# A hyperbolic attention layer: VectorE's per-unit flag, bound and product shifted one step ahead of its copies

## Chip, cores and metric

One Trainium2 chip, one core. The metric is the device time of one execution in microseconds (us). The kernel before ran three times: 2008.18, 2013.67 and 2014.71 us, median 2013.67.

## The reference

The input is x, 8 sequences of 1024 tokens with 256 features, in float32. The layer computes

```python
def _L0_attn_ref(x, W_q, W_k, W_v, W_o, log_c, beta, attention_bias):
    q_h = exp_map_at_origin(split_heads(x @ W_q.T), c)      # 16 heads of 16
    k_h = exp_map_at_origin(split_heads(x @ W_k.T), c)
    v_h = exp_map_at_origin(split_heads(x @ W_v.T), c)
    dist = poincare_distance(q_h, k_h, c)   # arccosh(max(1 + 2c|q-k|^2 / max((1-c|q|^2)(1-c|k|^2), EPS), 1 + EPS))
    weights = softmax(-beta_pos * dist - attention_bias)
    out = einsum('bhst,bhtd->bhsd', weights, log_map_at_origin(v_h, c))
    return concat(log_map_at_origin(exp_map_at_origin(out, c), c)) @ W_o.T
...
x = x + _L0_attn_ref(_layernorm(x), ...)
x = x + fp8_gemm(_layernorm(x)) + bias      # input and weights rounded to float8_e4m3
```

The denominator of the distance is bounded from below by EPS = 1e-5. For most pairs of head and tokens that bound is what holds, and then the distance depends on the product of q and k alone.

## The kernel before

**Steps and units.** The attention is cut into 512 steps. A group G (0 to 15) is 512 query tokens of one sequence; it has 32 steps s: 4 sets of 4 heads (hg) by 8 tiles of 128 keys (kt). Step n = 32 G + s computes one matrix of 128 keys by 4 x 512 queries. Four steps in a row are a unit. Before each unit ScalarE and VectorE each read a flag from `a.opens` into a register and branch on it. A unit whose flag is 0 is closed (the bound EPS holds for all its pairs), one whose flag is 1 is open. With these inputs 12 steps, three units, are open.

**ScalarE.** In a step it does a logarithm over 128x2048 (`log(n)`, L1053 from PSUM in a closed step, L1048 from SBUF in an open one) and, one step later in its order, an exponential (L1060) in place. Nothing else of weight runs on it in the loop.

**VectorE in an open step.** `bound(n)` (L1120, four operations of 128x512) writes the bounded factors into the ring U and counts up `m_rdy`; `clamp(n)` (L1129, 128x2048) multiplies them by the products of q and k in PSUM and counts up `freed`. `log(n)` waits for that, and so does TensorE with its next products. In a closed unit VectorE only counts `m_rdy` up by four.

**VectorE in every step.** It also copies what TensorE has put into PSUM bank 7 and works off pieces of two pipelines: `project` (layer norm, q, k, v and their maps, for a group two ahead) and `finish` (output projection and the fp8 layer, for the group before). Which piece belongs to which step is a table of slots: `PROJECT_USES` and `FINISH_USES` for the fills of bank 7, the `k ==` cases of the two `vector` functions for the pieces. Slots of `project` run four steps ahead of s, those of `finish` are s itself. So in groups 1 to 13 the steps 3 to 9 and 11 fill bank 7 with the products M0 to M7 (L394, copied by L481). Step 6 has the copy of M3 and then eleven short operations of `finish`, each of which waits for the one before (the last is L730). Steps 2, 10, 18 and 26 have the sums of a set of heads (`normalise`, L1143 to L1153). Step 18 has also the short pieces L609 to L613, step 19 the product L616. Step 22 ends in L750, which is waited for; step 23 copies R2 (L489) and then reduces A0 (filled by L404), both in bank 7, one behind the other.

**TensorE.** Its order in step n is: products of q and k for steps n+1 and n+2 (L947; they wait for `freed` of `log(n)`), first half of the step's fill of bank 7, the value products of step n-1 (L962), second half of the fill. Bank 7 is one bank: each fill waits until VectorE has copied the one before.

**The flag.** On VectorE it is this passage, once in four steps, between the pieces of a step with s = 3 modulo 4 and those of the next:

```python
o = opened(n0)
v.wait_ge(a.open_rdy, flags_of(n0))
hold(v, passed_v)
is_open = v.value_load(a.opens[0:1, o:o + 1], min_val=0, max_val=1)
with v.If(is_open > 0):
```

A group's flags are computed on VectorE itself, in step 27 of the group two earlier (step 2 for group 1, step 30 of group 0 for group 2). SyncE waits on `m_rdy` before it loads the factors of the next set of heads (`load_rq`, 1 MB, once in eight steps); closed steps don't read them.

Of the kernel before, what the change touches and what calls it, by code (L numbers as in the profile page):

```python
# [32 lines left out]
KT = S // P  # L33
# [6 lines left out]
STEPS = HG * KT  # L40
N = NG * STEPS
UNIT = 4
# [65 lines left out]
def hold(eng, passed):  # L108
    eng.sem_inc(passed, 1)
# [172 lines left out]
def at(table, slot, half):  # L282

    return [key for key, where in table.items() if where == (slot, half) or (half, where) == (1, (slot, BOTH))]
# [495 lines left out]
def emit_layer(nc, g):  # L780

    with ExitStack() as ctx:
# [24 lines left out]
        def in_step(G, s, half):  # L807

            found = []
            if s % KT == SUM_STEPS % KT and half == 0:  # L810
                x = HG * G + (s - SUM_STEPS) // KT
                if 0 <= x < NG * HG and G < NG:
                    found.append(("S", x // HG, x % HG))
            found += [(kind, n, i) for n, k in finished(G, s) for kind, i in at(FINISH_USES, k, half)]
            found += [(kind, n, i) for n, k in projected(G, s) for kind, i in at(project_uses(n), k, half)]
            if G == 0:
                found += [(kind, 1, i) for kind, i in at(FIRST_USES, s, half)]
            return found

        def projected(G, s):  # L820

            slots = [(2, k) for k in ([], [], [0, 1], [2, 3])[s]] if G == 0 and s < 4 else [(2, STEPS * G + s)]
            slots += [(n, STEPS * (G + 2 - n) + s + EARLY) for n in range(3, NG)]
            return [(n, k) for n, k in slots if 0 <= k < PROJECT_SLOTS]

        def project_uses(n):
            return SECOND_USES if n == 2 else PROJECT_USES

        def finished(G, s):

            return [(n, k) for n, k in ((G - 2, s + STEPS), (G - 1, s)) if n >= 0 and 0 <= k < FINISH_SLOTS]
# [14 lines left out]
        for key in tail:  # L846
            uses.add(key)

        project = project_stage(nc, ctx, g, a, uses)
        finish = finish_stage(nc, ctx, g, "fi_", on, a.b7_filled, a.b7_copied, uses)  # L850
        a.x1 = finish.xt
        flat = finish.sq[:, :, :, :].rearrange("p t h d -> p (t h d)")
        setup = setup_stage(nc, ctx, g, U[:, 0:2].rearrange("p r h q -> p (r h q)"), finish.xb[:, 0:2, :],
                            flat[:, 0:2 * D], flat[:, 2 * D:], finish.ocT[:, 0, :])
        KERNEL_STEP = 12

        def split(n):

            return n // STEPS, (n % STEPS) // KT, n % KT
# [5 lines left out]
        def place(n, h):  # L865

            return (h + 2) % HPG if n % 2 else h

        def chunk(n):
            return g.ps[:, 2 * (n % 2):2 * (n % 2) + 4, :].rearrange("p b n -> p (b n)")  # L870

        def opened(n):

            G, hg, kt = split(n)
            return (G * 2 + kt // UNIT) * HG + hg

        def flags_of(n):

            G, hg, kt = split(n)
            return max(G, 2 * (G // 2) + kt // UNIT) + 1  # L880

        with nc.Block() as block:
# [227 lines left out]
            def _(v):  # L1110
# [3 lines left out]
                def bound(n):  # L1114

                    G, hg, kt = split(n)
                    if n >= RING:
                        v.wait_ge(pv_done, n - RING + 1)
                    for h in range(HPG):
                        ins = v.tensor_scalar(U[:, n % RING, place(n, h), :], rqb[:, h, :],  # L1120
                                              a.rk[:, (G // 2) % 2, hg * HPG + h, kt:kt + 1],
                                              1.0 / EPS, ALU.mult, ALU.min)
                    ins.then_inc(m_rdy, 1)

                def clamp(n):
                    v.wait_ge(m_rdy, n + 1)
                    v.wait_ge(d_rdy, n + 1)
                    all4 = U[:, n % RING].rearrange("p b n -> p (b n)")
                    v.tensor_tensor(all4, all4, chunk(n), ALU.mult).then_inc(freed, 1)  # L1129

                def copy_sums(x):
                    v.wait_ge(pv_done, KT * (x + 1))
                    if x >= 1:
                        v.wait_ge(a.b7_filled, uses.after(("S", (x - 1) // HG, (x - 1) % HG)))
                    v.tensor_copy(OTs[:, :], g.ps[:, 6, :]).then_inc(ot_done, 1)  # L1135

                def normalise(G, hg):
                    x = HG * G + hg
                    step = Steps(v, sum_steps, 2 * x)
                    pairs = g.ps[:, 7, :].rearrange("p (a r) -> p a r", r=2 * VW)  # L1140
                    sums = pairs[:, :, DH:DH + 2 * NS].rearrange("p a (b r) -> p a b r", b=2)
                    v.wait_ge(a.b7_filled, uses.after(("S", G, hg)))
                    step(v.tensor_reduce(den[:, :].rearrange("p (a b) -> p a b", b=2), sums, AX.X, ALU.add))  # L1143
                    v.tensor_reduce(cm[:, x:x + 1], pairs[:, :, DH:DH + 2 * NS], AX.XY, ALU.max)
                    step(v.reciprocal(den[:, :], den[:, :]))
                    for odd in range(2):
                        v.tensor_tensor(on[:, :, hg * HPG + odd:(hg + 1) * HPG:2, :],
                                        pairs[:, :, odd * (2 * VW - DH):odd * (2 * VW - DH) + DH].rearrange(
                                            "p (t c) r -> p t c r", t=GT),
                                        den[:, odd::2].rearrange("p (t c) -> p t c", t=GT).unsqueeze(3).broadcast_to(  # L1150
                                            [P, GT, HPG // 2, DH]), ALU.mult).then_inc(on_done, 1)
                    v.wait_ge(on_done, 2 * x + 2)
                    v.sem_inc(a.b7_copied, 1)  # L1153

                def copy(kind, n, i):
                    if kind == "S":
                        normalise(n, i)
                    elif (kind, i) in FINISH_USES:
                        finish.copy(v, n, (kind, i))
                    else:  # L1160
                        project.copy(v, n, (kind, i))

                def unit(n0, is_open):
                    for n in range(n0, n0 + UNIT):
                        G, s = n // STEPS, n % STEPS
                        if is_open and n + 1 < n0 + UNIT:
                            bound(n + 1)
                            clamp(n + 1)
                        for key in in_step(G, s, 0):
                            copy(*key)  # L1170
                        for key in in_step(G, s, 1):
                            copy(*key)
                        if n % KT == 0 and n >= KT:
                            copy_sums(n // KT - 1)
                        for m, k in finished(G, s):
                            finish.vector(v, m, k)
                        for m, k in projected(G, s):
                            project.vector(v, m, k)
                        if n == KERNEL_STEP:
                            setup.vector_kernel(v)  # L1180

                for k in range(3):
                    project.vector(v, 0, k, first)
# [7 lines left out]
                for n0 in range(0, N, UNIT):  # L1191
# [3 lines that stand above are left out]
                    is_open = v.value_load(a.opens[0:1, o:o + 1], min_val=0, max_val=1)  # L1195
                    with v.If(is_open > 0):
                        v.wait_ge(rqb_in, 16 * (n0 // KT + 1))
                        bound(n0)
                        clamp(n0)
                        unit(n0, True)  # L1200
                    with v.Else():
                        v.sem_inc(m_rdy, UNIT)
                        unit(n0, False)
                copy_sums(NG * HG - 1)
                normalise(LAST, HG - 1)
                for m, k in after:
# [262 lines left out]
```

## Time and profile before

| | |
|---|---|
| median of three runs | 2013.67 us |
| the profiled execution, its own time | 2004.81 us |
| its span, first to last instruction | 2003.0 us |
| mean granted TensorE clock | 0.973 |
| ScalarE busy | 1871.1 us, 93% |
| TensorE (matmul) busy | 1776.1 us, 89% |
| VectorE busy | 1139.9 us, 57% |
| start of the first and of the last logarithm (L1053) | 45.2 and 1942.8 us |

The span runs from the first instruction to the last; the execution's own time is 1.8 us longer. Shares are means over the span. An engine can be busy for 57% of it and still be what the others wait for in some steps.

### The profile page before, as it was taken

To read this page: it belongs to the slowest core of one execution; us is meant where nothing else is said; L and a number is where in the kernel's file an instruction comes from. 1 tells how busy PE (TensorE), PEld (TensorE's weight loads), DVE (VectorE), ACT (ScalarE), POOL (GpSimd) and SP (SyncE) were. 2 spreads that over 40 slices of the span, in tenths; PEclk is the share of its full clock that TensorE was granted. 3 is DMA by queue.
4 is the path that set the end of the run, shared out by engine and by line. 5 is a ranking of instruction groups with operands and counts; after the bars stand their busy time and mean duration, and the time that the engine had idled before them with its cause. 6 is when DMAs were issued, how large, how long until landed. Compare 5 with 4: busy or idle time off the path is not lost. (4 is left out here: it accounts for less than half of the span.)

```text
span 2003.0 us, 29496 instructions
## 1 busy us (share of the span) xinstructions
PE 1776.1 (89%) x10689; PEld 593.9 (30%) x10689; DVE 1139.9 (57%) x2813; ACT 1871.1 (93%) x1090; POOL 14.3 (1%) x35
## 2 busy tenths in 40 slices
PE   7888989999898798989898898999989899999982
PEld 4222322323232232323222232232323223333321
DVE  7463665655565765655657666565656556323435
ACT  5799999999999699999998999999999999999990
POOL 2000000000000000000000000000000000000000
PEclk9799999999999899999999999999999999999995
DMA  1323122041313114122030412204131220412001
GB/s 56 111 93 106 46 97 79 22 133 43 118 37 101 53 43 133 27 96 75 25 130 22 133 43 87 89 23 133 43 113 42 101 64 22 123 43 64 22 22 32
DMA packets 112937, 142.53 MB, mean 71 GB/s; under 512 B 35676, under 2 KB 61533, under 8 KB 112733
## 3 DMA queue, kind: packets, MB, share of 16 engines
q1 hardware_dynamic: 112732, 140.13, 22.2%
q8 instruction: 89, 1.46, 0.3%
q14 instruction: 116, 0.94, 0.2%
HBM read 85.07 MB, written 55.05 MB: 70 GB/s over the span
## 5 line engine op out<-in xcount | busy, mean ns | idle before, releaser
L1060 ACT ACTIVATE U<-U 128x2048 f32<-128x2048 f32 x512 | 1003.1, 1961 | 0.3
L1053 ACT ACTIVATE U<-ps 128x2048 f32<-128x2048 f32 x500 | 961.8, 1924 | 29.6 <-PE ps L947 22.6
L947 PE MATMUL ps<-q_T,k_T 18*128 18x512 f32 x4096 | 628.0, 644 | 134.4 <-ACT U L1053 108.8
L962 PE MATMUL ps<-U,vals 128*32 128x512 f32 x4096 | 555.0, 614 | 29.2 <-ACT U L1060 28.9
L947 PEld LDWEIGHTS ps<-q_T,k_T 18*128 18x128 f32 x4096 | 196.7, 185 | 349.9 <-ACT U L1053 274.2
L394 PE MATMUL ps<-wT,xnT 128*128 128x384 f32 x512 | 228.1, 537 | 4.7 <-DVEq L1153 2.5
L481 DVE COPY qkv<-ps 128x384 f32<-128x384 f32 x112 | 62.4, 557 | 220.0 <-PE ps L394 220.0
L962 PEld LDWEIGHTS ps<-U,vals 128*32 128x32 f32 x4096 | 81.2, 109 | 197.4 <-ACT U L1060 136.8
L985 PE MATMUL ps<-woT,ident 128*128 128x256 f32 x396 | 138.9, 432 | 0.0
L394 PEld LDWEIGHTS ps<-wT,xnT 128*128 128x128 f32 x512 | 79.4, 190 | 194.6 <-issue 109.5
L399 PE MATMUL ps<-ident,rows 128*128 128x128 f32 x512 | 106.6, 305 | 5.9 <-DVE rows L616 3.6
L489 DVE COPY q_T<-ps 128x512 f32<-128x512 f32 x60 | 41.5, 691 | 120.3 <-PE ps L399 120.3
L399 PEld LDWEIGHTS ps<-ident,rows 128*128 128x128 f32 x512 | 54.0, 144 | 179.5 <-issue 129.9
L985 PEld LDWEIGHTS ps<-woT,ident 128*128 128x128 f32 x396 | 59.1, 188 | 159.1 <-issue 146.2
L491 DVE COPY k_T<-ps 128x512 f32<-128x512 f32 x60 | 41.5, 691 | 69.9 <-PE ps L399 69.6
L1135 DVE COPY OTs<-ps 128x512 f32<-128x512 f32 x64 | 43.8, 684 | 65.3 <-PE ps L962 65.3
L682 PE MATMUL ps<-woT,fi_ocT 128*128 128x256 f32 x256 | 75.4, 421 | 1.6 <-DVE fi_ocT L704 0.8
L1143 DVE TENSOR_REDUCE den<-ps 128x16 f32<-128x256 f32 x64 | 27.2, 424 | 70.7 <-PE ps L971 70.1
L682 PEld LDWEIGHTS ps<-woT,fi_ocT 128*128 128x128 f32 x256 | 45.7, 198 | 54.8 <-issue 25.1
L710 DVE TENSOR_TENSOR fi_x<-fi_xt,ps 128x512 f32<-128x512 f32 x32 | 22.0, 688 | 64.8 <-PE ps L682 64.8
L572 DVE TENSOR_REDUCE ss<-sqr 128x48 f32<-128x768 f32 x56 | 53.4, 953 | 1.9
L571 DVE TENSOR_TENSOR sqr<-qkv 128x768 f32<-128x768 f32 x56 | 53.1, 948 | 0.0
(178 smaller groups left out, 1138.5 us busy)
## 6 DMA issues: line engine op xcount, KB each, us to landing
rqb<-q_scratch SPq DMA_DIRECT2D x64, 1024.0 KB, 5.6
q_scratch<-q_T SPq DMA_DIRECT2D x16, 1024.0 KB, 4.6
k_scratch<-k_T SPq DMA_DIRECT2D x16, 1024.0 KB, 6.8
v_scratch<-vals SPq DMA_DIRECT2D x16, 768.0 KB, 10.8
fi_xt<-in_L_attn_x_dram SPq DMA_DIRECT2D x17, 512.0 KB, 5.5
out_dram<-fi_x SPq DMA_DIRECT2D x16, 512.0 KB, 3.9
xt<-in_L_attn_x_dram SPq DMA_DIRECT2D x15, 512.0 KB, 6.2
rk_scratch<-rk SPq DMA_DIRECT2D x16, 32.0 KB, 12.0
```

The lines of the kernel that those rows point to most:

```text
L394: ins = pe.matmul(bank[:, 0:384], xnT[:, dc, t * P:(t + 1) * P], g.wT[:, dc, half * 384:(half + 1) * 384], start=dc == 0, stop=dc == 1)
L399: ins = pe.transpose(bank[:, t * P:(t + 1) * P], rows[:, qk, t, hg * HPG:(hg + 1) * HPG, :].rearrange("p h r -> p (h r)"), g.ident[:, :])
L481: v.tensor_copy(qkv[:, t, 24 * half:24 * (half + 1), :].rearrange("p h d -> p (h d)"), bank[:, 0:384]).then_inc(a.b7_copied, 1)
L571: step(v.tensor_tensor(sqr[:, :], src, src, ALU.mult))
L572: step(v.tensor_reduce(ss[:, t, :], sqr[:, :].rearrange("p (h d) -> p h d", d=DH), AX.X, ALU.add))
L682: ins = pe.matmul(bank[:, a * D:(a + 1) * D], ocT[:, dc, t * P:(t + 1) * P], g.woT[:, dc, :], start=dc == 0, stop=dc == 1)
L947: ins = pe.matmul(g.ps[:, 2 * pair + i, :], a.k_T[HB * h:HB * h + RD, b % 2, hg, kt * P:(kt + 1) * P], a.q_T[HB * h:HB * h + RD, G % 3, hg ...
L962: ins = pe.matmul(g.ps[HB * h:HB * h + VW, 6, :], a.vals[:, b % 2, kt, (hg * HPG + h) // 2, DH * (h % 2):DH * (h % 2) + VW], U[:, n % RING ...
L985: pe.matmul(g.ps[:, 7, 0:D], g.ident[:, :], g.woT[:, 0, :], start=True, stop=True)
L1053: act.activation(U[:, n % RING].rearrange("p b n -> p (b n)"), chunk(n), ACT.Ln, scale=-2.0 / EPS, bias=1.0).then_inc(freed, 1)
L1060: act.activation(U[:, n % RING], U[:, n % RING], ACT.Exp, scale=exponent).then_inc(exp_done, 1)
L1135: v.tensor_copy(OTs[:, :], g.ps[:, 6, :]).then_inc(ot_done, 1)
```

## The change

Before, a unit did for each of its steps n: bound and product of n+1, then the copies and pieces of n; bound and product of the unit's first step came right behind the flag. After, it does for each n: bound and product of n, then the copies and pieces of n-1 (`rest(n - 1)`). So the copies and pieces of a unit's last step are issued behind the flag of the next unit, and in an open unit behind its first bound and product too. A closed unit does the same without bound and product: its flag and the count of `m_rdy` now stand ahead of the pieces of the step before the unit. The operations are the same, and each piece keeps its place among the pieces. The last step's pieces follow the loop.

```
+                def rest(n):
+                    G, s = n // STEPS, n % STEPS
+                    for key in in_step(G, s, 0):
+                        copy(*key)
+                    for key in in_step(G, s, 1):
+                        copy(*key)
+                    if n % KT == 0 and n >= KT:
+                        copy_sums(n // KT - 1)
+                    for m, k in finished(G, s):
+                        finish.vector(v, m, k)
+                    for m, k in projected(G, s):
+                        project.vector(v, m, k)
+                    if n == KERNEL_STEP:
+                        setup.vector_kernel(v)
                 def unit(n0, is_open):
                     for n in range(n0, n0 + UNIT):
-                        G, s = n // STEPS, n % STEPS
-                        if is_open and n + 1 < n0 + UNIT:
-                            bound(n + 1)
-                            clamp(n + 1)
...
+                        if is_open:
+                            bound(n)
+                            clamp(n)
+                        if n:
+                            rest(n - 1)
...
                     with v.If(is_open > 0):
                         v.wait_ge(rqb_in, 16 * (n0 // KT + 1))
-                        bound(n0)
-                        clamp(n0)
                         unit(n0, True)
                     with v.Else():
                         v.sem_inc(m_rdy, UNIT)
                         unit(n0, False)
+                rest(N - 1)
                 copy_sums(NG * HG - 1)
```

## Rows read from the trace of the kernel before

**Rows 1.** The page, part 1: busy time, share, instructions of each engine.
```profile
PE 1776.1 (89%) x10689; PEld 593.9 (30%) x10689; DVE 1139.9 (57%) x2813; ACT 1871.1 (93%) x1090; POOL 14.3 (1%) x35
```

**Rows 2.** Groups of instructions of ScalarE (busy, mean ns, idle before).
```profile
L1053 ACT ACTIVATE U<-ps 128x2048 f32<-128x2048 f32 x500 | 961.8, 1924 | 29.6 <-PE ps L947 22.6
L1048 ACT ACTIVATE U<-U 128x2048 f32<-128x2048 f32 x12 | 22.9, 1912 | 26.3 <-DVE U L1129 26.2
```

**Rows 3.** Timeline, ScalarE, steps 164 to 168 (start, duration; idle before in brackets).
```profile
668.04 1.91 ACT L1048 ACTIVATE U<-U 128x2048 f32<-128x2048 f32 x1 [7.27 <-DVE U L1129]
...
689.12 1.88 ACT L1053 ACTIVATE U<-ps 128x2048 f32<-128x2048 f32 x1
```

**Rows 4.** The same stretch on VectorE.
```profile
661.19 0.56 DVE L481 COPY qkv<-ps 128x384 f32<-128x384 f32 x1 [4.09 <-PE ps L394]
...
664.01 1.67 DVE L1120 TENSOR_SCALAR U<-rqb,rk 128x512 f32<-128x512 f32 x4 [1.14 <-issue]
665.72 2.29 DVE L1129 TENSOR_TENSOR U<-U,ps 128x2048 f32<-128x2048 f32 x1
...
670.26 2.29 DVE L1129 TENSOR_TENSOR U<-U,ps 128x2048 f32<-128x2048 f32 x1 [0.66 <-PE ps L947]
...
674.90 0.56 DVE L481 COPY qkv<-ps 128x384 f32<-128x384 f32 x1 [2.35 <-PE ps L394]
```

**Rows 5.** The same stretch on TensorE.
```profile
668.07 2.19 PE L947 MATMUL ps<-q_T,k_T 18*128 18x512 f32 x8 [6.91 <-DVE U L1129]
```

**Rows 6.** Timeline, VectorE, at the other two open units (steps 276 and 492).
```profile
1078.92 0.49 DVE L1147 TENSOR_TENSOR on<-ps,den 128x128 f32<-128x128 f32 x2
...
1082.55 1.67 DVE L1120 TENSOR_SCALAR U<-rqb,rk 128x512 f32<-128x512 f32 x4
...
1870.18 1.68 DVE L1120 TENSOR_SCALAR U<-rqb,rk 128x512 f32<-128x512 f32 x4 [1.04 <-issue]
```

**Rows 7.** Timeline, VectorE, first operation behind a closed flag, four places.
```profile
1169.23 0.56 DVE L481 COPY qkv<-ps 128x384 f32<-128x384 f32 x1 [1.57 <-PE ps L394]
...
1728.28 1.22 DVE L725 TENSOR_REDUCE fi_oss<-fi_osq 128x64 f32<-128x1024 f32 x1 [1.25 <-issue]
...
1843.56 1.22 DVE L725 TENSOR_REDUCE fi_oss<-fi_osq 128x64 f32<-128x1024 f32 x1 [1.56 <-issue]
...
1903.06 1.40 DVE L739 BATCH_NORM_STATS2 fi_stats<-fi_x 128x6 f32<-128x256 f32 x4 [1.16 <-issue]
```

**Rows 8.** Timeline, all engines, group 6, steps 6 to 8.
```profile
807.08 0.25 DVE L730 TENSOR_SCALAR fi_oy<-fi_oy,sc 128x64 f32<-128x64 f32 x1
...
807.62 1.14 PE L947 MATMUL ps<-q_T,k_T 18*128 18x512 f32 x8
807.79 0.56 DVE L481 COPY qkv<-ps 128x384 f32<-128x384 f32 x1 [0.46 <-PE ps L394]
...
808.69 0.91 PE L394 MATMUL ps<-wT,xnT 128*128 128x384 f32 x2
808.79 1.88 ACT L1053 ACTIVATE U<-ps 128x2048 f32<-128x2048 f32 x1
```

**Rows 9.** Timeline, all engines, group 6, steps 22 to 24.
```profile
862.27 1.37 DVE L750 TENSOR_SCALAR fi_xb<-fi_x,fi_mv,fi_rstd 128x256 bf16<-128x256 f32 x4
...
863.83 0.69 DVE L489 COPY q_T<-ps 128x512 f32<-128x512 f32 x1 [0.18 <-PE ps L399]
...
864.69 0.28 PE L404 MATMUL ps<-ident,amax 128*32 128x128 f32 x1
...
865.46 1.24 PE L947 MATMUL ps<-q_T,k_T 18*128 18x512 f32 x8 [0.48 <-ACT U L1053]
...
867.05 1.93 ACT L1053 ACTIVATE U<-ps 128x2048 f32<-128x2048 f32 x1
```

**Rows 10.** Timeline, group 0, steps 3 to 6.
```profile
76.60 0.41 PE L390 MATMUL ps<-ident,xt 128*128 128x128 f32 x2 [1.73 <-DVE xt L564]
...
81.06 1.88 ACT L1053 ACTIVATE U<-ps 128x2048 f32<-128x2048 f32 x1 [2.48 <-PE ps L947]
```

More of the change, by code:

```diff
@@ L1161, in copy @@
                         project.copy(v, n, (kind, i))
+                def rest(n):
[12 more added lines that the diff above has]
+                        setup.vector_kernel(v)
                 def unit(n0, is_open):
                     for n in range(n0, n0 + UNIT):
-                        G, s = n // STEPS, n % STEPS
-                        if is_open and n + 1 < n0 + UNIT:
-                            bound(n + 1)
-                            clamp(n + 1)
[L1169 to L1180, printed above, removed]
+                        if is_open:
[3 more added lines that the diff above has]
+                            rest(n - 1)
                 for k in range(3):
```

## The prediction

> **What bounds the kernel now.** I read the page first: ScalarE is busy for 93% of the span, TensorE for 89%, VectorE for 57% [rows 1]. The groups of ScalarE say what it waits for: in 500 closed steps 29.6 us in all, mostly for TensorE, but in the 12 open steps 26.3 us, for VectorE's product [rows 2]. So ScalarE sets the pace, and the open units are where VectorE stops it. Then I laid out the timeline step by step. Most steps are limited by ScalarE alone. In the steps that fill M products TensorE has more to do than ScalarE and runs without a gap, and the logarithm follows the start of L947 by a fixed 1.17 us (807.62 to 808.79) [rows 8]. There any delay of TensorE goes straight to the end, since ScalarE never makes time good.
>
> I cost the change by place: three open units, where the product comes earlier, and some 125 closed flags, where only the flag moves.
>
> **What a flag costs.** Where nothing else hides it, VectorE stands still behind a closed flag for 1.25 us (L723 ended at 1727.03, L725 began at 1728.28), 1.56, 1.57 and 1.16 us [rows 7]; the last includes a semaphore of the sums. Behind an open flag it is 1.14 us [rows 4] and 1.04 us [rows 6]. If the operation ahead of the flag isn't waited for, the flag passes beneath it: at step 276 bound follows L616 without a gap [rows 6]. If it is waited for, the whole flag is exposed. I take 1.25 to 1.57 us, middle 1.40, and 1.05 as the low bound. The Trainium skill (Advanced Engine Details and Errata, Control Flow Timing) gives a compare-and-branch about 108 ns; Runtime: NRT & Kernel Launch, Instruction fetch mechanics, says that a taken branch whose target is out of the window stalls for a fetch. By the first figure alone moving the flag would be free; the rows are ten times that and fit the second rule better, though no row shows the fetch itself.
>
> **The open unit at step 164 (gain).** VectorE was done with step 162 at 657.10 (661.19 less the 4.09 it then waited for M0), and ScalarE was free at 660.77 (668.04 less 7.27) [rows 3, 4]. After the change flag, bound (1.71) and product (2.29) start at 657.10, and the product ends near 662.2, not 668.01. Its products of q and k are there, since TensorE has issued them ahead of M0. From there on VectorE is the bound of the unit, and what it saves is its own waiting: 4.09 for M0, 0.66 for L947 and 2.35 for the next M, together 7.1 us [rows 4]; its work stays the same and lies back to back. TensorE, which had stood still for 6.91 us and came back at half clock (L947 took 2.19 us) [rows 5], has all the fills ready in time. Term: -7.1 us. Bounds: -7.5, and -5 if TensorE still falls to half clock within the unit and makes VectorE wait for a fill.
>
> **Step 276 (small loss).** Here VectorE had no waits ahead of bound. L616, which hid the flag, now comes behind it, and the flag stands ahead of it behind the sums (ended 1079.41) and the five short operations of step 274, during which it can run; from 1079.5 on its 1.04 to 1.57 us end near 1081.0 [rows 6, 7], about 0.6 after the last of the five (an estimate from the timeline between these rows). The product comes 1.5 us sooner for the first step, but the work is back to back as before and has gained a gap of about 0.6 us. Term: +0.6, bounds +0.2 and +0.8. **Step 492:** step 491 has no copies and no pieces, so order and times stay: 0.
>
> **The start (loss).** In group 0 the first X fill of step 4 waits for L564 of step 3, and TensorE's wait (1.73 us) becomes a wait of ScalarE (2.48 us) [rows 10]. The flag of unit 4 now stands ahead of step 3's copy and L564, behind a chain of waited operations that ran without a pause. The full flag is added: +1.3, bounds +1.0 and +1.5.
>
> **Step 7 of groups 1 to 13, without 5 (the large loss).** The flag of the unit that begins at 8 moves from behind step 7 to between steps 6 and 7. Step 6 ends in L730 at 807.33, waited for. The copy of M4 began at 807.79, when its fill was there; TensorE wants it done by 808.69 [rows 8]. With the flag it begins at 807.33 + 1.25 to 1.57 = 808.58 to 808.90, ends 0.56 later, and TensorE goes on 0.06 after that (668.01 to 668.07 [rows 4, 5]): 809.20 to 809.52 against 808.69. That is 0.51 to 0.83 us in a chain with no slack; middle 0.65, twelve times: +7.8 us. With 1.05 it is 12 x 0.31 = 3.7, with 1.57 it is 10.0. At the old place the flag was just covered: at 1169.23 a copy started late because of it, ended at 1169.79, and the next M fill started on time [rows 7]. In group 5 the pieces of step 6 lie in the open unit, and the fill is then as late as the copy.
>
> **Step 23 of the same groups, without 8 (loss).** The flag of unit 24 moves between L750, waited for until 863.64, and the copy of R2, which began at 863.83. It now begins at 864.89 to 865.21 and ends 0.69 later; A0 (L404), which began at 864.69, can begin at 865.64 to 865.96. L947 follows L404's start by 0.29 at least (865.46 less its wait of 0.48, less 864.69), and the logarithm by 1.17 more: 867.10 to 867.42 against 867.05 [rows 9]. So 0.05 to 0.37, middle 0.2, twelve times: +2.4; bounds 0 and 4.4.
>
> **The other flags: 0.** The new places are ahead of the steps with s = 3, 11, 15, 19, 27 and 31. At 3, 11 and 27 the next copy waits for its fill today, behind work that ends early (4.09 us at s = 3 [rows 4], which covers the 1.57); at 19 the next fill is two steps away; at 15 and 31 the work ahead isn't waited for and hides most of the flag. If that cover were gone, a copy would be 0.4 us late where TensorE has 0.3 to 0.4 us of slack. The old places gave no stall to win back. SyncE's loads of factors can start a step sooner, as `m_rdy` counts sooner; nobody in a closed step reads them. The copy of the sums isn't moved past a longer queue.
>
> **Sum.** -7.1 + 0.6 + 0 + 1.3 + 7.8 + 2.4 = +5.0 us. On the profiled execution's 2004.8 us that is 2009.8; the median of the runs lies 8.9 us above that execution, so I forecast 2013.7 + 5.0 = 2018.7 us. All bounds together give -2.6 to +11.7.
>
> **Rivals.**
> First, the flag is cheap at the new places and the change does what its first look says: faster. It needs less than 0.74 us behind L730 (808.69 less 807.33, less copy and semaphore); then step 7 and step 23 cost nothing, and -7.1 + 0.6 + 0.5 leaves -6.0 us, 2007.7. The clean unit of step 164 speaks for it; four closed flags of 1.16 to 1.57 us against it [rows 7]. Chance 0.09. The Trainium skill's 108 ns (Advanced Engine Details and Errata, Control Flow Timing) would put the flag below that point.
> Second, every flag falls on the upper value, step 23 leaks in full, and part of the gain at 164 goes to the half clock: -6 + 0.8 + 1.5 + 10.0 + 4.4 = +10.7, 2024.4. For it: two of four closed flags are at 1.56 or more [rows 7], and the clock fell in this unit before [rows 5]. Against it: the other two. Chance 0.33 for everything over +6.
> Third, flags and gain cancel or nothing moves at all (-2 to +2): 0.2. The forecast itself, +2 to +6: 0.38.
>
> **How the numbers follow.** A measurement of this kernel tells 0.3%, 6 us, from no change. Faster by more is the first rival, 0.09. Slower by more is the second, 0.33. Between lie the forecast and the third, 0.58. The range 2010.5 to 2024.5 (-3 to +11) takes in the bounds of the sum but not the first rival and the worst of the second. The forecast's own range is 2015.7 to 2019.7.
>
> **What would show it.** Step 164: L1048 begins 1.4 to 1.8 us after ScalarE was free, not 7.27, and step 168 comes 7 us sooner relative to step 163. Step 276: first product sooner, third one 0.6 us later. Group 0: L564 over 1 us later behind L263. Groups of steps: the logarithm of step 9 comes 0.5 to 0.8 us later than before, relative to step 3, in twelve groups, with L394 waiting for the copy L481, and a gap of 1.25 us or more between L730 and L481. L404 about 1 us later in step 23. It is wrong if the gap behind L730 is under 0.74 us, if TensorE catches up before step 11, or if the clock falls at new places.

## The result, and the profile of the changed kernel

| | before | after |
|---|---|---|
| median of 10 runs each, us | 2012.31 (2007.91 to 2014.71) | 2021.41 (2015.66 to 2023.24) |
| ratio of the times | | 1.0045, 95% interval 1.0033 to 1.0056 |
| profiled execution, span, us | 2003.0 | 2019.4 |
| its mean granted clock | 0.973 | 0.967 |

The changed kernel is slower, by 9.1 us between the medians. The forecast was +5.0 us, 2018.7, within a range up to 2024.5: the sign and the range were right, the size was not. The forecast's own narrower range, 2015.7 to 2019.7, was missed, and the time lies where the second rival had put it.

The page of the profile after, part 1 (engine, busy us, share of the span, instructions), beside [rows 1]:
```profile
PE 1790.7 (89%) x10689; PEld 597.1 (30%) x10689; DVE 1141.7 (57%) x2813; ACT 1872.9 (93%) x1090; POOL 14.6 (1%) x35
```
Every engine has as many instructions as before and ScalarE and VectorE are as long busy. Only TensorE's time grew, by 14.6 us: more of it ran at half clock. What changed is where ScalarE stood still. Its groups of instructions after (busy us, mean ns, then idle before), beside [rows 2]:
```profile
L1053 ACT ACTIVATE U<-ps 128x2048 f32<-128x2048 f32 x500 | 956.9, 1914 | 48.1 <-PE ps L947 41.9
L1048 ACT ACTIVATE U<-U 128x2048 f32<-128x2048 f32 x12 | 22.9, 1911 | 21.3 <-DVE U L1129 21.3
```
In the open steps its wait for VectorE's product fell from 26.3 to 21.3 us; in the closed steps its wait, almost all for L947's scores, rose from 29.6 to 48.1. The gain is there, and something more than three times as large stands against it.

To see where, I took the intervals between the starts of ScalarE's 512 first passes (L1053, or L1048 in an open step) in both traces and subtracted them step by step. The interval of step n is the time from the start of its first pass to that of step n+1. Four places carry it all: the intervals of steps 8 to 10 of twelve groups (nearly all of it in that of step 9), the interval of step 24 in four groups, the three open units with the steps behind them, and the start with group 0.

**Step 164.** Timeline after, ScalarE, VectorE and TensorE together (start, duration; idle before in brackets), beside [rows 3 to 5]:
```profile
670.10 1.68 DVE L1120 TENSOR_SCALAR U<-rqb,rk 128x512 f32<-128x512 f32 x4 [1.04 <-issue]
671.81 2.29 DVE L1129 TENSOR_TENSOR U<-U,ps 128x2048 f32<-128x2048 f32 x1
674.02 0.55 DVE L481 COPY qkv<-ps 128x384 f32<-128x384 f32 x1
674.13 1.91 ACT L1048 ACTIVATE U<-U 128x2048 f32<-128x2048 f32 x1 [1.39 <-DVE U L1129]
...
685.65 1.66 PE L947 MATMUL ps<-q_T,k_T 18*128 18x512 f32 x8 [1.94 <-DVE U L1129]
...
691.98 1.91 ACT L1048 ACTIVATE U<-U 128x2048 f32<-128x2048 f32 x1 [2.50 <-DVE U L1129]
692.26 2.09 PE L947 MATMUL ps<-q_T,k_T 18*128 18x512 f32 x8
...
699.41 0.56 DVE L481 COPY qkv<-ps 128x384 f32<-128x384 f32 x1 [3.76 <-PE ps L394]
...
700.80 1.88 ACT L1053 ACTIVATE U<-ps 128x2048 f32<-128x2048 f32 x1 [2.75 <-PE ps L947]
```
ScalarE now waits 1.39 us where it waited 7.27, and VectorE's copy of M0 follows the product without its pause of 4.09 us. But a batch of L947 took 2.09 us at 692.26 and the passes behind the unit wait for TensorE, 2.75 us at 700.80. The stretches (core time; each engine's busy us; then the granted clock) say why:
```profile
670.00:686.00 16.00, 11.31 (x61) 3.43 (x60) 15.69 (x22) 10.77 (x7) 0.00 (x0) 1.00 0.10 35
686.00:700.00 14.00, 14.00 (x44) 3.51 (x42) 9.38 (x22) 9.04 (x5) 0.00 (x0) 0.51 0.25 75
700.00:1090.00 390.00, 356.78 (x2206) 116.61 (x2200) 231.94 (x573) 384.27 (x218) 0.00 (x0) 1.00 0.22 71
```
From 686 to 700 us TensorE had 0.51 of its clock, the level of 1.2 GHz, and was busy for all of the 14 us; ahead of it, within the unit, it had stood still for 1.04 and 1.94 us at a time before L947. The prediction had named a clock that falls at new places as a sign of being wrong. Before, this group's half clock had ended at 688.0 us, 1.1 us ahead of step 168's logarithm [rows 3]; here it ends at 700.0, 5.6 us behind that logarithm, and ScalarE pays for it. Of group 5's gain of 7.4 us by the shift (a second execution, below) this profile shows 4.0.

**Step 7.** Timeline after, group 6, beside [rows 8]:
```profile
815.29 0.26 DVE L730 TENSOR_SCALAR fi_oy<-fi_oy,sc 128x64 f32<-128x64 f32 x1
...
815.83 1.14 PE L947 MATMUL ps<-q_T,k_T 18*128 18x512 f32 x8
816.79 0.56 DVE L481 COPY qkv<-ps 128x384 f32<-128x384 f32 x1 [1.25 <-PE ps L394]
817.01 1.88 ACT L1053 ACTIVATE U<-ps 128x2048 f32<-128x2048 f32 x1
...
817.41 0.91 PE L394 MATMUL ps<-wT,xnT 128*128 128x384 f32 x2 [0.43 <-DVE qkv L481]
...
821.26 1.88 ACT L1053 ACTIVATE U<-ps 128x2048 f32<-128x2048 f32 x1 [0.58 <-PE ps L947]
```
The idle time of VectorE ahead of the copy is 1.25 us instead of 0.46, TensorE waits 0.43 us for the copy where it had not waited, and the next logarithm, that of step 10, waits 0.58 us for the scores. The copy's row names TensorE's fill (L394) as releaser, but that fill had ended at 815.90, 0.89 us earlier; what ended last is the flag. The rows for the same place in groups 2, 3, 4, 8, 9 and 10 read 1.56 to 1.64 with "issue" as the releaser.

**Step 23.** Timeline after, group 6, beside [rows 9]:
```profile
871.00 1.37 DVE L750 TENSOR_SCALAR fi_xb<-fi_x,fi_mv,fi_rstd 128x256 bf16<-128x256 f32 x4
...
873.94 0.69 DVE L489 COPY q_T<-ps 128x512 f32<-128x512 f32 x1 [1.56 <-issue]
...
874.68 0.28 PE L404 MATMUL ps<-ident,amax 128*32 128x128 f32 x1 [1.20 <-DVE q_T L489]
874.89 1.14 PE L947 MATMUL ps<-q_T,k_T 18*128 18x512 f32 x8
...
876.07 1.88 ACT L1053 ACTIVATE U<-ps 128x2048 f32<-128x2048 f32 x1
```
Here VectorE stands still for 1.56 us, and L404 waits 1.20 us for the copy. The interval to the pass at 876.07 grew by 0.3 us.

### The profile page after: what moved, and what is told of

Its sections match the earlier page's. It is cut to its first block and busy times, and to the rows that moved or that the text cites. A ratio compares the mean times of both kernels' runs of the same rounds, so it can differ in the third digit from the quotient of the medians.

```text
span 2019.4 us, 29494 instructions
## 1 busy us (share of the span) xinstructions
PE 1790.7 (89%) x10689; PEld 597.1 (30%) x10689; DVE 1141.7 (57%) x2813; ACT 1872.9 (93%) x1090; POOL 14.6 (1%) x35
## 5 line engine op out<-in xcount | busy, mean ns | idle before, releaser
L1053 ACT ACTIVATE U<-ps 128x2048 f32<-128x2048 f32 x500 | 956.9, 1914 | 48.1 <-PE ps L947 41.9
L947 PE MATMUL ps<-q_T,k_T 18*128 18x512 f32 x4096 | 633.0, 650 | 120.1 <-ACT U L1053 102.0
L947 PEld LDWEIGHTS ps<-q_T,k_T 18*128 18x128 f32 x4096 | 196.7, 186 | 336.3 <-ACT U L1053 264.6
L394 PE MATMUL ps<-wT,xnT 128*128 128x384 f32 x512 | 232.8, 547 | 12.4 <-DVE qkv L481 7.5
L394 PEld LDWEIGHTS ps<-wT,xnT 128*128 128x128 f32 x512 | 81.2, 194 | 205.9 <-issue 114.0
```

Of the source, the lines that this page charges most:

```text
L394: ins = pe.matmul(bank[:, 0:384], xnT[:, dc, t * P:(t + 1) * P], g.wT[:, dc, half * 384:(half + 1) * 384], start=dc == 0, stop=dc == 1)
L947: ins = pe.matmul(g.ps[:, 2 * pair + i, :], a.k_T[HB * h:HB * h + RD, b % 2, hg, kt * P:(kt + 1) * P], a.q_T[HB * h:HB * h + RD, G % 3, hg ...
L1053: act.activation(U[:, n % RING].rearrange("p b n -> p (b n)"), chunk(n), ACT.Ln, scale=-2.0 / EPS, bias=1.0).then_inc(freed, 1)
```

## The experiments

All kernels take the changed kernel and add a rule for which units are shifted; a unit not shifted has the old order. The common edit:
```
+                def shifted(n0):
+                    G, s = n0 // STEPS, n0 % STEPS
+                    return <rule>
...
-                        if n:
+                        if n > n0 or (n and shifted(n0)):
                             rest(n - 1)
+                    if n0 + UNIT < N and not shifted(n0 + UNIT):
+                        rest(n0 + UNIT - 1)
```
Times below are read in two ways. The ratio is to the kernel before in the same series. And because the granted clock of every run is known, each kernel's mean is also set against a straight line through 56 runs of the kernel before (2004.0 to 2015.7 us, clock 0.965 to 0.973): mean 2011.4 us at 0.9684, and 1.13 us longer for each 0.001 of clock less, with 1.3 us of scatter left. "At equal clock" is a kernel's mean distance from this line, with two standard errors of that mean alone. The line takes off every difference of clock, also one that the change itself makes, and what low clock costs depends on where it falls; so at equal clock a kernel's own effect on the clock is hidden. For the changed kernel's ten runs (mean 2020.6 us, clock 0.9668) it is +7.5 ± 0.8 us; the other 1.8 us of its distance to the line's mean are clock.

**1. Only the unit that begins at step 8 is shifted.** Rule: `return s == 8 and G >= 1`.

> The order of the kernel before, with the flag moved ahead of one step's pieces at one place alone: the unit that begins at step 8, in groups 1 to 15. Theory (the flag stands exposed between L730 and the copy of M4): 12 groups lose 0.5 to 0.85 us each, +6 to +10 us against before, and the logarithm of step 9 is the place. Rival (the loss of the changed kernel comes from the clock and the start, not from this flag): within 2 us of before.

Measured: median 2017.93 us, ratio 1.0026 (1.0014 to 1.0037); at equal clock +8.7 ± 0.5. VectorE, group 6, step 7:
```profile
811.21 0.26 DVE L730 TENSOR_SCALAR fi_oy<-fi_oy,sc 128x64 f32<-128x64 f32 x1
812.73 0.56 DVE L481 COPY qkv<-ps 128x384 f32<-128x384 f32 x1 [1.26 <-PE ps L394]
```
The same 1.26 us, and the intervals of steps 8 to 10 grew by 8.1 us in the same twelve groups. Eleven of them grew by the amounts of the changed kernel or within 0.1 us of them; group 8 grew by 0.53 instead of 0.83, with an idle time of 1.27 instead of 1.58. Group 5, where the prediction had seen no loss, grew by 0.6. The ratio says less than that, because these runs had more clock (0.9702) than those of before beside them (0.9673). The loss is this flag's.

**2. Only the unit that begins at step 4 is shifted.** Rule: `return s == 4 and G >= 1`.

> The shift at the unit that begins at step 4 alone, in groups 1 to 15; step 164 is one of these. Theory: the open unit gains 4 to 7 us (6.7 up to its fourth step, less what a half clock behind it takes), the closed ones cost nothing, since the copy of M0 waits for its fill: -4 to -7 us. Rival (any moved flag costs, or the gain is given back behind the unit): -1 to +2 us.

Measured: median 2002.57 us, ratio 0.9946 (0.9932 to 0.9959), so faster than before by 0.54%; at equal clock -5.6 ± 1.2. In the trace group 5 is 7.2 us shorter and the closed flags at step 3 of the other groups cost nothing. ScalarE in the open unit and behind it:
```profile
665.06 1.91 ACT L1048 ACTIVATE U<-U 128x2048 f32<-128x2048 f32 x1 [1.41 <-DVE U L1129]
670.69 1.91 ACT L1048 ACTIVATE U<-U 128x2048 f32<-128x2048 f32 x1 [1.78 <-DVE U L1129]
676.54 1.91 ACT L1048 ACTIVATE U<-U 128x2048 f32<-128x2048 f32 x1 [2.00 <-DVE U L1129]
682.90 1.91 ACT L1048 ACTIVATE U<-U 128x2048 f32<-128x2048 f32 x1 [2.50 <-DVE U L1129]
684.78 1.88 ACT L1053 ACTIVATE U<-ps 128x2048 f32<-128x2048 f32 x1
```
The unit's waits are those of the changed kernel to 0.02 us, and nothing is lost behind it. The rest of the gain is clock: these runs had 0.9713. The traces say where some of it comes from. In group 5, in the nine kernels that keep the old order at step 164, TensorE ran 17.1 us at half clock (13.7 in one); in the five executions with that unit shifted it was 3.4, 3.4, 6.8, 6.8 (this one) and 13.7. TensorE no longer stands still for 6.9 us there. Ten us of half clock less are 0.0025 of the mean clock, an estimate from these stretches, against the 0.0029 measured here; so the shift itself gives most of this clock, and the -5.6 at equal clock, which takes it off, says less than the 7.2 us of the trace.

**3. All units but the one at step 8 are shifted.** Rule: `return not (G >= 1 and s == 8)`.

> The changed kernel with the old order at the unit that begins at step 8 alone (groups 1 to 15). Theory: it gets back the 6 to 10 us: -1 to +4 us against before. Rival: it stays at +7 to +11 us like the changed kernel.

Measured: median 2009.46 us, ratio 0.9984 (0.9975 to 0.9993); at equal clock -1.1 ± 1.2. The intervals of steps 8 to 10 are unchanged in all groups. With experiment 1 the two halves give 8.7 - 1.1 = +7.6, against +7.5 for the whole: at equal clock the change is their sum. The plain ratios, 1.0026 and 0.9984, add up to 1.0010 only, against 1.0045; the sum rests on the line.

**4. All but the units at step 8, at step 24 and the second of group 0.** Rule: `return not (G >= 1 and s in (8, 24)) and n0 != 4`.

> As the one before, and the old order also at the unit that begins at step 24 (groups 1 to 15) and at unit 4 of group 0. Theory: another 1.3 us for the start and 1 to 2 for step 23, so -5 to +1 us against before. Rival (start and step 23 cost nothing): the same as the one before, within 1 us.

Measured: median 2002.05 us, ratio 0.9941 (0.9928 to 0.9954); at equal clock -5.8 ± 1.3. The fastest version with experiment 2, and no different from it: the other flags are free, and give nothing either. In the trace 7.2 us are gone in group 5, step 276 costs 0.33 and the intervals of step 24 are unchanged. Experiment 3 less this one is 4.6 us at equal clock, of which its trace shows 1.3 for step 23, and the start's flag takes 1.3 (below); the uncertainty of the difference is 1.7, so some 2 us stay over.

**5. The old order, built by the same rule.** Rule: `return False`.

> Every unit in the old order, with the steps' remaining work in a helper: the instructions of the kernel before, only the lines and the last steps' place in the program differ. Both theories expect the ratio within 0.2% of 1.000 (2010 to 2018 us) and, in the trace, every step interval of groups 1 to 15 the same as before except where TensorE's granted clock falls. What the intervals of the two traces differ by here, with no shifted unit, is what the clock and a second execution alone do; the losses found at steps 7 of groups 1 to 13 have to be absent.

Measured: median 2011.59 us, ratio 1.0005 (0.9989 to 1.0021); at equal clock 0.0 ± 1.1. Its last pass began 8.2 us later than in the profile of before, though the order is the same: 2.6 us ahead of the first step, 1.8 in group 0, 3.7 in group 8. Everywhere else the intervals agree to 0.3 us. Groups 0 and 8 had more low clock than in the profile of before (the 2.6 us ahead of the first step are not explained by it), here around step 276:
```profile
1090.00:1100.00 10.00, 9.06 (x34) 2.62 (x38) 9.31 (x20) 7.65 (x4) 0.00 (x0) 0.58 0.00 0
1100.00:1125.00 25.00, 20.95 (x111) 5.99 (x103) 17.56 (x35) 17.91 (x10) 0.00 (x0) 0.76 0.14 43
```
So the difference of two profiles of this kernel carries 8 us of chance at the start and in groups 0 and 8 alone, and what I had put down to the change there can't be read from the profile after.

**6. Only the second unit of group 0 is shifted.** Rule: `return n0 == 4`.

> Only the unit at step 4 of group 0 is shifted. By my terms +1.0 to +1.5 us and nothing else, ratio 1.0005 to 1.0008, so under what the timing tells; in the trace the interval of step 5 of group 0 grows by about 1.0 to 1.3 us beside old_order_again. The rival, that the shift at the start moves TensorE's half clock stretches of group 0 and costs several us: +3 to +6 us, ratio 1.0015 to 1.003, with longer stretches at half clock before 130 us.

Measured: median 2012.47 us, ratio 1.0013 (1.0002 to 1.0025); at equal clock +1.2 ± 0.7. In the trace the flag costs what the term said: the copy ahead of L564 comes after 1.29 us of idle time, and L564 begins 2.07 us behind L263's start where it had been 0.80. VectorE and ScalarE:
```profile
76.10 0.69 DVE L491 COPY k_T<-ps 128x512 f32<-128x512 f32 x1 [1.29 <-issue]
...
83.42 1.88 ACT L1053 ACTIVATE U<-ps 128x2048 f32<-128x2048 f32 x1 [4.47 <-PE ps L947]
```
But ScalarE's wait behind it is 4.47 us against 2.48 [rows 10], and the stretch from 77 to 91 us, first in the profile of before, then here, had another clock:
```profile
77.00:91.00 14.00, 13.24 (x79) 3.96 (x78) 2.56 (x4) 11.52 (x7) 0.00 (x0) 0.88 0.34 110
77.00:91.00 14.00, 12.77 (x51) 3.15 (x52) 2.46 (x6) 8.08 (x6) 0.00 (x0) 0.51 0.36 114
```
The intervals of steps 5 to 9 of group 0 grew by 4.3 us beside before, not by 1.3. That is the rival's mechanism, and the plain ratio, +0.4 to +5.0 us, holds the term as well as most of the rival; the +1.2 can't decide, since it takes off just the clock that the rival speaks of. In the traces group 0 moves by as much between kernels that don't shift this unit (experiment 4 has +6.3 us there beside before, experiment 1 has -0.7), so one execution doesn't decide either. The flag's own 1.3 us is shown; what the shift costs through the clock stays open.

**7. The changed kernel a second time**, for its trace.

> The changed kernel a second time, for its trace. What belongs to the change stays: the interval of step 8 of groups 1 to 4 and 6 to 13 longer by 0.5 to 0.9 us each (+8.4 in sum), step 23 by 0.3 in four groups, the unit at step 164 shorter by 6.7. What belongs to TensorE's clock may move: the stretches at half clock of the start and of group 0, the 2.7 us lost behind the unit at step 164, the 2 us at step 276 and the 2 us at step 492. If the 2.7 us behind step 164 are there again, they belong to the shifted order and not to chance; only the closed flag at step 8 of group 5 then distinguishes this kernel from those in which they were absent.

Measured: one execution, 2013.28 us with a span of 2011.5 at clock 0.972, which is +6.0 us at equal clock (one run scatters by 1.3 about the line). Its intervals at steps 8 to 10 of the twelve groups and at step 24 of the four are those of the first trace to 0.02 us. Beside the first profile it is 4.6 us shorter in group 0 and 3.4 in group 5. The stretch behind step 164:
```profile
667.00:683.00 16.00, 11.32 (x60) 3.53 (x52) 15.79 (x19) 10.74 (x7) 0.00 (x0) 0.96 0.00 1
683.00:697.00 14.00, 12.81 (x62) 3.34 (x60) 10.89 (x24) 11.33 (x7) 0.00 (x0) 0.92 0.23 75
```
0.92 in place of 0.51, with the same waits of ScalarE within the unit (1.39, 1.78, 2.00 and 2.50 us). The loss behind the unit was this execution's clock and not a part of the order. Group 5 gives 7.4 us here.

**8 to 12. What the flag's price is made of.** A flag is, on VectorE, a wait for the count of flags, a semaphore increment, a load of one word from SBUF into a register and a branch over the unit's open body; the closed body begins with another increment. Five kernels keep the old order and put parts of this ahead of the copy of M4 in step 7, where [rows 8] give a place without slack. Nothing is left out of the computation.
8, an increment and a load without a branch, at the start of `rest(n)`:
```
+                    if s == 7 and G >= 1:
+                        hold(v, passed_v)
+                        v.value_load(a.opens[0:1, 0:1], min_val=0, max_val=1)
```

> The old order, and in addition, ahead of the fourth copy of step 7 of groups 1 to 15, VectorE waits for GpSimd's flag and loads it from SBUF into a register, without a branch. Theory A (the wait and the load are the larger part of the 0.7 to 1.1 us that a closed flag takes VectorE): the idle time of VectorE behind L730 at group 6's step 7 rises from 0.46 us towards 0.9 to 1.2, TensorE's next fill starts as much later, and the sum over 13 groups is +4 to +8 us, 2016 to 2022. Theory B (the branch and the fetch of its target are the larger part): idle time under 0.7 us, sum under +2.5 us, 2012 to 2016.

9, a short branch alone, on the register `now[0]` that the unit before has loaded:
```
+                    if s == 7 and G >= 1:
+                        with v.If(now[0] > 0):
+                            hold(v, passed_v)
```

> The old order, and in addition, at the same place, a compare and branch on the flag register that the unit of before has already loaded; no new load from SBUF, and a body of one wait. Theory A (load is the cost): idle time of VectorE behind L730 stays under 0.7 us, sum of the 13 groups under +2.5 us, 2012 to 2016. Theory B (branch is the cost): idle time 0.9 to 1.2 us, sum +4 to +8 us, 2016 to 2022. Both may show parts: then the two runs' excesses should add to the excess of the shifted flag (0.79 us at group 6).

10, load and short branch:
```
+                    if s == 7 and G >= 1 and G != 5:
+                        hold(v, passed_v)
+                        o = opened(n - 3)
+                        now[0] = v.value_load(a.opens[0:1, o:o + 1], min_val=0, max_val=1)
+                        with v.If(now[0] > 0):
+                            for _ in range(1):
+                                v.wait_ge(a.open_rdy, 1)
```

> The old order, and ahead of the fourth copy of step 7 of groups 1 to 15 but 5, VectorE loads a closed flag from SBUF into a register and branches on it over a body of one instruction. Seen so far at group 6, from the end of L730 to the copy: 0.46 us without either (the copy waits for TensorE's fill), 0.76 with a load alone, 0.39 with a short branch alone, 1.25 with the shifted flag. Theory C (what is missing, 0.4 to 0.5 us, is the distance of the jump, over a body of some hundred instructions): 0.75 to 0.9 us here and no growth of the step intervals. Theory D (load and branch in a row are dear in themselves, since the branch has to wait for the loaded value): 1.1 to 1.3 us here and the intervals of step 7 grow by 0.3 to 0.8 us in each of 13 groups.

11, load and long branch, the same with `range(160)`:

> The same with a body of 160 waits in place of one. It should be the shifted flag's own price: 1.1 to 1.3 us from L730 to the copy, and the interval of step 7 longer by 0.4 to 0.85 us in each of the 13 groups, by both theories. If it stays at 0.8, neither theory holds, and the price lies in what the shifted order has besides (the Else body, other code behind).

12, long branch alone, as 11 without the three lines of the load:

> The same long body without a load: the branch is on the register that the unit before has loaded. Theory C: 0.5 to 0.8 us from L730 to the copy (0.4 to 0.5 for the jump and the branch's own few hundredths, of which up to 0.4 lay behind TensorE's fill before), no growth of the intervals or under 0.1 us. Theory D: 0.39 to 0.46 us, as with the short body.

(In 8, 10 and 11 there is an increment ahead of the load, and in none of them the wait that the expectation of 8 names; 9 and 12 have no increment ahead of the branch. The flag isn't GpSimd's: VectorE computes it and waits for its own count.) VectorE at the copy of group 6, first 8:
```profile
812.33 0.26 DVE L730 TENSOR_SCALAR fi_oy<-fi_oy,sc 128x64 f32<-128x64 f32 x1
813.34 0.56 DVE L481 COPY qkv<-ps 128x384 f32<-128x384 f32 x1 [0.76 <-PE ps L394]
```
9:
```profile
813.53 0.56 DVE L481 COPY qkv<-ps 128x384 f32<-128x384 f32 x1 [0.39 <-PE ps L394]
```
10, with TensorE's next fill:
```profile
814.11 0.56 DVE L481 COPY qkv<-ps 128x384 f32<-128x384 f32 x1 [0.97 <-PE ps L394]
814.72 0.91 PE L394 MATMUL ps<-wT,xnT 128*128 128x384 f32 x2 [0.15 <-DVE qkv L481]
```
11:
```profile
812.37 0.56 DVE L481 COPY qkv<-ps 128x384 f32<-128x384 f32 x1 [0.96 <-PE ps L394]
```
11, the same place in group 7:
```profile
927.53 0.25 DVE L730 TENSOR_SCALAR fi_oy<-fi_oy,sc 128x64 f32<-128x64 f32 x1
929.05 0.56 DVE L481 COPY qkv<-ps 128x384 f32<-128x384 f32 x1 [1.26 <-PE ps L394]
```
12:
```profile
811.08 0.56 DVE L481 COPY qkv<-ps 128x384 f32<-128x384 f32 x1 [0.55 <-PE ps L394]
```

| ahead of the copy | idle at group 6, us | idle in the twelve groups, us | intervals of steps 8 to 10, all groups but 5, us |
|---|---|---|---|
| nothing (5) | 0.46 | 0.46 | 0.0 |
| short branch (9) | 0.39 | 0.39 | 0.0 |
| long branch (12) | 0.55 | 0.39 in three, 0.55 in nine | +0.1 |
| increment and load (8) | 0.76 | 0.76 | +1.7 |
| the same and short branch (10) | 0.97 | 0.96 in ten, 1.34 in two | +4.3 |
| the same and long branch (11) | 0.96 | 0.97 in six, 1.27 in six | +6.3 |
| the shifted flag (after) | 1.25 | 1.25 in six, 1.58 in six | +8.4 |

The increment and the load together are the larger part: they alone take the idle time from under the fill's 0.46 to 0.76. No run has the increment alone, so the two aren't taken apart. A branch on a loaded register hides under 0.46, and adds 0.2 behind a fresh load. The length of the body shows over the groups. With the load alone, and with the short branch alone, all twelve groups have one value. The long body has two: 0.16 us apart when it is alone, 0.3 us apart behind a load, and the shifted flag has the same two steps 0.3 us higher. Group 6 lies on the lower step in 11 and in the changed kernel, so it shows nothing of it.

In 8 the idle time, 0.76, falls between the theories; the load alone costs 1.7 us, as B had it, and not 4 to 8. 9 went as A said. For 10, C had 0.75 to 0.9 us and no growth, D had 1.1 to 1.3; ten groups show 0.96 with 0.2 to 0.5 us of growth, two show 1.34 with 0.6, so both miss. For 11 both had 1.1 to 1.3, which holds in six of twelve groups. For 12, C's 0.5 to 0.8 holds in nine. The last 0.3 us, from 0.97 to 1.25 and from 1.27 to 1.58, lie in what the shifted flag has besides, the wait for the count of flags and the closed body's start; no run takes them apart. Timed, 8 gave a ratio of 1.0008 (0.9997 to 1.0019) and 9 of 1.0020 (1.0006 to 1.0033), at equal clock +2.2 ± 1.0 and +1.4 ± 0.6. The first is its trace's 1.7; for the second the trace has 0.3 us in steps outside the low clock and 0.4 at step 492, so some 0.7 us is unexplained. 10, 11 and 12 ran once each: 2015.85, 2018.75 and 2012.26 us at clocks of 0.970, 0.971 and 0.970, at equal clock +6.4, +10.4 and +2.8, where one run scatters by 1.3. Their traces give 4.3, 10.6 and 1.5 with the stalls told of in the last section.

## Why the prediction was right in sign and short in size

**Step 164, -7.1.** Right in mechanism and size: -7.2 in experiments 2 and 4 and -7.4 in the second trace of after. L1048 waited 1.39 us where 1.4 to 1.8 had been named. The profile shown above has only -4.0 because of its half clock. That was the lower bound's case and beyond it: the clock fell at 686 us, within the unit, but the unit's waits stayed as they were, and the loss of 3.4 us came behind it, where ScalarE waited for TensorE.

**Step 7, +7.8.** Right in mechanism and nearly in size: 8.4 us. The idle time behind L730 was 1.25 to 1.27 or 1.56 to 1.64 us in the twelve groups, as [rows 7] had it for other places, with 1.64 the longest; the intervals grew by 0.50 to 0.52 in five groups and by 0.81 to 0.90 in seven, where the working had given 0.51 and 0.83. The idle times are six of each; that the mean is 0.70 and not the middle of 0.65 is owed to group 10 (0.90 at 1.64) and to group 11, which lost 0.87 with an idle time of 1.26, which I can't explain. The place is one step off: the logarithm that comes late is that of step 10, not of step 9, which in group 6 follows an L947 that had started before the late fill. Group 5, which the prediction left out, lost 0.6 in experiment 1, but nothing in the second trace of after. Experiment 1, with this flag alone, gave +8.7 at equal clock.

**Step 23, +2.4.** Half: 1.2 us. Only where the flag took 1.55 us or more did anything come through, and there 0.3 us, in groups 5, 6, 11 and 12; with 1.25 the delay vanished, so L947 has some 0.05 us more room behind L404 than the wait of 0.48 suggested.

**The start, +1.3, step 276, +0.6.** The start's flag is 1.3 us in the trace of experiment 6, and 1.2 ± 0.7 came of it at equal clock; what it costs besides, through the clock, is open. Step 276 is 0.33 in both traces of after: the gap ahead of bound was 0.24 us and not 0.6. The row behind the start's flag in the profile after, VectorE:
```profile
79.24 0.69 DVE L491 COPY k_T<-ps 128x512 f32<-128x512 f32 x1 [1.28 <-issue]
```
**Step 492, 0.** Not quite: the open flag took 1.41 us at its new place where it had taken 1.04, and the interval is 0.37 longer in both traces. That the order stays does not keep the flag's own price. Experiment 9, which has the old order there but other code ahead, shows 1.42 us at this flag and the same 0.37, so it goes with where the code lies. VectorE, profile after:
```profile
1886.71 1.68 DVE L1120 TENSOR_SCALAR U<-rqb,rk 128x512 f32<-128x512 f32 x4 [1.41 <-issue]
```
**The other flags, 0.** Right: experiments 2 and 4 shift all or most of them and their intervals are those of before.

**The sum, the step that failed.** By measured terms it is -7.4 + 8.4 + 1.2 + 1.2 + 0.3 + 0.4 = +4.1 us, less 0.4 that steps 5 to 7 of the closed groups gave back in both traces, some 0.07 at a time: +3.7, so the sum of +5.0 was not short of what the trace shows step by step. The runs say +7.5 at equal clock and +9.1 between medians. What the prediction lacked is a term for TensorE's clock outside of its own places: it treated the half clock only as a bound of step 164 and as "part of the gain" in a rival. Ten runs had 0.9668 against 0.9684, which is 1.8 us by the line. The other 3.8 us (7.5 less 3.7) stay open. Experiment 3 has a gap of the same kind (its steps add to some -4.3 us, the runs say -1.1), experiment 2 a smaller one (-7.2 and -5.6); experiments 1, 4 and 6 have 0.7 us or less. Two things can hold it, and neither is shown. The line takes off the clock that the shift at step 164 gives, though ScalarE was waiting for VectorE there and most of it gained no time; that makes kernels with this shift look slower by 3 to 4 us at most (an estimate: 10 to 14 us of half clock are 0.0025 to 0.0035 of the mean clock, at 1.13 us per 0.001), but in experiment 4 there is little of it. And low clock costs more where TensorE sets the pace: the profile after lost 3.4 us in group 5 that the second trace did not lose, and the start's shift may move the half clock of group 0 (experiment 6). That the forecast's sign came out rests on its terms; that the measured 9.1 us lies within the range is owed to the width of the bounds, for the steps alone give 3.7. The second rival named the size, but not for its reason: half of the flags were on the lower value and step 23 leaked 1.2 of 4.4 us.

**The rules.** The first rival, that the flag is cheap, fell: it needed less than 0.74 us behind L730 and the row shows 1.25. The 108 ns that the Trainium skill gives a compare-and-branch (Advanced Engine Details and Errata, Control Flow Timing) may hold for a branch alone: experiment 9 shows no delay by one where under 0.46 us is hidden, and experiment 10 shows 0.2 us of it behind a fresh load; but it isn't the price of a flag, of which increment and load are the larger part. The fetch stall that the Trainium skill names for a far branch (Runtime: NRT & Kernel Launch, Instruction fetch mechanics) was taken in the prediction for the main cost; here the longer body alone showed 0.16 us in nine groups of twelve, and behind a load 0.3 us in six of them, so as the explanation of the 1.25 us it was wrong. It may be what lies between 1.25 and 1.58, since that step depends on the place and hardly shows without a long jump (in two groups of twelve, experiment 10); no row shows a fetch.

## What to carry to other kernels

Before a flag or any load into a register is moved, look at what the engine's next operation releases: the closed flags here cost 1.25 to 1.6 us of VectorE where the operation ahead was waited for, and the open flag at step 276, where it was not, cost nothing before. Moving one shared pattern everywhere pays for one place with all the others; shift only the unit that gains (here step 4's), and the kernel is 0.54% faster (0.28% at equal clock) in place of 0.45% slower. And read small changes against the granted clock of each run: the line through the runs of before took the scatter from some 3 us to 1.3.

## What the hardware showed that I had not expected

**A flag has two prices, by its place in the program.** In both traces of the changed kernel, in which the same step lies 5 to 8 us apart, the same groups read 1.25 (1, 6, 7, 11, 12, 13) and the same 1.56 to 1.64 us (2, 3, 4, 8, 9, 10) at step 7. It is no chance of an execution. In experiment 1, with other code around the same flags, group 8 has the lower value and group 11 the higher, and in experiment 11 the higher ones are 2, 4, 7, 9, 11 and 13; so it goes with the layout of the program and not with the group's work.

**Branches add stalls elsewhere.** With the long body and the load (experiment 11) VectorE stood still for 3.79 us ahead of a copy of step 5 in group 6, released by nothing the profile shows, and ScalarE waited 1.45 us for it:
```profile
800.89 0.56 DVE L481 COPY qkv<-ps 128x384 f32<-128x384 f32 x1 [3.79 <-issue]
...
805.36 1.88 ACT L1053 ACTIVATE U<-ps 128x2048 f32<-128x2048 f32 x1 [1.45 <-PE ps L947]
```
Intervals 1.4 us longer stand in groups 1, 6 and 8 of experiment 11 and in group 9 of experiment 12, in none of the other kernels. 160 more instructions of VectorE lie ahead of it in the program, so a late fetch fits, but the trace has no row of one.

**The clock is worth as much as the change.** The same kernel took 2004.0 us at 0.973 and 2015.7 us at 0.965.
